# Prediction: maxima, shift and router a step sooner in a fused attention and expert kernel

## What is computed

```python
x = x + cross_attention(layernorm(x), ctx, ctx)   # 16 heads of 16, 1601 keys a batch, biases
x = x + causal_attention(layernorm(x))            # 16 heads, 64 positions a batch
x = x + experts(layernorm(x))                     # 8 experts, 256 -> 1024 -> 256, gelu
```

## Time and profile before

| what | value |
|---|---|
| median of 3 runs | 737.78 us (737.48 to 739.73) |
| the profiled execution | 738.75 us, span 736.7 us |
| granted TensorE clock, mean | 0.958 |
| TensorE busy | 668.6 us (91%) |
| VectorE busy | 498.7 us (68%) |
| ScalarE busy | 325.4 us (44%) |
| GpSimd busy | 226.2 us (31%) |

### The profile page before, as it was taken

The page is one execution under the profiler, slowest core; times in us unless marked ns, Lnnn a source line. Parts: engine busy times, 40 slices in busy tenths (PEclk is TensorE's granted clock), DMA queues, the critical chain, the costliest instruction groups (busy, mean ns, idle before and its releaser), DMA issues.

```text
span 736.7 us, 16650 instructions
## 1 busy us (share of the span) xinstructions
PE 668.6 (91%) x6576; PEld 549.2 (75%) x6584; DVE 498.7 (68%) x868; ACT 325.4 (44%) x517; POOL 226.2 (31%) x111
## 2 busy tenths in 40 slices
PE   2969999999999968999997999976897999999997
PEld 2648878878778846876885886654766898999996
DVE  4785687886748774774877757477556766676663
ACT  2434555554444533445453443445235443434431
POOL 2004566665535643643654644200000000000000
PEclk9988999999999988999998998999797999999999
DMA  6120120110110010001000000031400233112000
GB/s 227 58 68 2 25 67 24 27 44 24 25 44 24 24 26 23 23 24 46 24 24 23 2 1 2 1 116 40 189 1 1 115 115 116 69 45 114 0 0 28
DMA packets 12501, 34.16 MB, mean 46 GB/s; under 512 B 1483, under 2 KB 9812, under 8 KB 10260
## 3 DMA queue, kind: packets, MB, share of 16 engines
q1 hardware_dynamic: 12180, 31.62, 12.9%
q0 software_dynamic: 256, 1.58, 0.6%
HBM read 32.67 MB, written 0.52 MB: 45 GB/s over the span
## 4 chain that ended last, share of the span: by engine, by line
PE 79%; DVE 14%; issue 3%; ACT 2%; DMA 1%; SPq 0%; DVEq 0%; POOL 0%; ACTq 0%
PE bank L1015 44%; PE bank L1179 13%; PE bank L1024 8%; PE bank L1075 4%; DVE maxes L762 4%; PE bank L1118 2%; DVE ctx_lo L703 2%; PE bank L1109 2%; DMA bias_sb<-in_biases 1%; PE bank L1093 1%; ACT probs L638 1%; DVE shift L721 1%; DVE prob_sum L431 1%; DVE ties L810 1%; DVE masked L711 1%
## 5 line engine op out<-in xcount | busy, mean ns | idle before, releaser
L431 POOL TENSOR_TENSOR prob_sum<-probs,prob_sum 128x1024 f32<-128x1024 f32 x84 | 203.4, 2421 | 150.1 <-ACT probs L638 149.3
L638 ACT ACTIVATE probs<-bank 128x1024 f32<-128x1024 f32 (+1 forms) x104 | 106.6, 1025 | 140.4 <-PE bank L1179 137.2
L762 DVE TENSOR_REDUCE maxes<-bank 128x1 f32<-128x400 f32 (+1 forms) x256 | 131.5, 564 | 22.2 <-PE bank L1075 20.3
L620 ACT ACTIVATE h_raw<-bank,b_sb 128x512 f32<-128x512 f32 (+1 forms) x72 | 46.2, 642 | 106.8 <-PE bank L1015 106.7
L744 DVE SCALAR_TENSOR_TENSOR k_lo<-bank,bias_sb,k_hi 128x400 fp32r<-128x400 f32 (+2 forms) x64 | 40.5, 632 | 58.5 <-ACT k_hi L541 58.4
L1179 PE MATMUL bank<-qbd_hi,k_hi 64*128 64x256 f32 (+1 forms) x416 | 72.6, 343 | 7.5 <-issue 4.1
L1015 PE MATMUL bank<-w_hi,h_hi 128*128 128x256 f32 x256 | 72.9, 285 | 0.2 <-DVE h_lo L962 0.2
L1015 PE MATMUL bank<-w_hi,h_lo 128*128 128x256 f32 x256 | 72.6, 284 | 0.0
L1015 PE MATMUL bank<-w_lo,h_hi 128*128 128x256 f32 x256 | 72.5, 283 | 0.0
L961 DVE CAST h_hi<-h_raw 128x512 fp32r<-128x512 f32 (+1 forms) x72 | 28.5, 396 | 63.5 <-ACT h_raw L620 63.1
L1024 PE MATMUL bank<-probs,v_sb 128*32 128x128 f32 (+1 forms) x1664 | 69.1, 285 | 2.5 <-DVE masked L711 2.0
(11 more groups left out here) (157 smaller groups left out, 1452.2 us busy)
## 6 DMA issues: line engine op xcount, KB each, us to landing
raw<-in_w SPq DMA_DIRECT2D x16, 1024.0 KB, 6.8
ctx_raw<-in_ctx_t SPq DMA_DIRECT2D x16, 400.0 KB, 3.6
ctx_raw<-in_ctx_t SPq DMA_DIRECT2D x8, 402.0 KB, 3.6
ctx_raw<-in_ctx_t SPq DMA_DIRECT2D x8, 399.0 KB, 3.6
w_sb<-in_w_t POOLq DMA_DIRECT2D x1, 1280.0 KB, 9.5
x_all<-in_x SPq DMA_DIRECT2D x1, 512.0 KB, 3.8
w_raw<-in_w_t SPq DMA_DIRECT2D x1, 512.0 KB, 4.9
result<-x_all SPq DMA_DIRECT2D x1, 512.0 KB, 2.7
```

Source lines behind the costliest of these rows:

```text
L431: engine.tensor_tensor(prob_sum[0:ROWS[k], :], probs[0:ROWS[k], s % 2, :], acc[0:ROWS[k]], ALU.add).then_inc(summed, 1)
L620: nc.scalar.activation(h_raw[:, c % 2, 0:width], bank[:, at, 0:width], ACT.Gelu, bias=b1_sb[:, bass.ds(e, 1), c:c + 1].rearrange("p a b -> ...
L638: nc.scalar.activation(probs[0:ROWS[k], s % 2, :].rearrange("p (g n) -> p g n", g=G), bank[0:ROWS[k], 0:ROW_TILES, :], ACT.Exp, scale=SCAL ...
L762: nc.vector.tensor_reduce(maxes[:, g * PAIRS + j, c:c + 1], src[:, 0:width], AX.X, ALU.max).then_inc(read_dve, 1)
```

## The change

Three tables and one condition. The maxima of the next batch end with step 9 instead of 10: one pair fewer in step 10, one more in step 2. `find_shift` is worked at the start of VectorE's step 10 (k = KT - 3) instead of 11; X stays in step 12. In the middle tiles `y2` moves from step 19 to 18, `xt2` from 21 to 20, `router` from 22 to 21, and with them what follows on each: statistics, inverse root, normalisation, split, `row_max`, `route`. `gt` stays in step 24. Since one line is added, lines behind line 81 carry a number higher by one in the changed kernel.

```diff
-M_AT = in_order({1: 2, 2: 1, 3: 2, 4: 1, 5: 2, 6: 2, 7: 1, 8: 2, 9: 2, 10: 1})
+M_AT = in_order({1: 2, 2: 2, 3: 2, 4: 1, 5: 2, 6: 2, 7: 1, 8: 2, 9: 2})
...
 SHIFT_AT = KT - 1
+FIND_SHIFT_AT = KT - 3
...
-            15: ["o0"], 16: ["o1"], 19: ["y2"], 21: ["xt2"], 22: ["router"], 24: ["gt"], 25: ["b2"]}
+            15: ["o0"], 16: ["o1"], 18: ["y2"], 20: ["xt2"], 21: ["router"], 24: ["gt"], 25: ["b2"]}
...
-                    if k == SHIFT_AT - 1 and more > bi:
+                    if k == FIND_SHIFT_AT and more > bi:
```

## The result

The changed kernel takes **736.03 us** (median of 22 runs, 732.90 to 738.29). The kernel before, run beside it, takes 738.66 us (22 runs, 737.26 to 741.19). The ratio is 0.9959 with a 95% interval of 0.9948 to 0.9971: about 3.0 us less, where 2.0 were forecast. The interval begins and ends on the faster side, at 0.3 to 0.5%.

What follows compares the result with a forecast made beforehand. TensorE bounds the kernel, idling at gt for gates whose VectorE route GpSimd's sums hold. Middle tiles gain 2.4 us, step 3 costs 0.4: 2.0 us less, 737.78 to 735.8 us (chance 0.45), range 732.0 to 738.6.

Steps and rivals of the forecast that it cites:

- rival 1: Middle tiles: L810 wins the heat, one sum fewer holds the route; 4.6 us in all, 733.2 us; chance 0.22.
- rival 2: Middle tiles: the route meets no sum and the wait goes; 6.2 us a tile, 725.8 us; chance 0.05.
- rival 3: Middle tiles: moving ctx_lo costs what the route gains, scores of step 12 stay at 270.6; 738.2 us; chance 0.16.
- rival 4: Middle tiles: row_max comes 2.4 us late, a fourth sum holds the gates; each tile 1.2 later, 740.6 us; chance 0.12.
- The price of the pair at step 3: First pair of step 3 needs keys step 2 just made; 0.1 us in each of four batches, +0.4 us.
- the 0.29 us that the pair gives back ahead of step 10: TensorE's time for a pair of maxima ahead of step 10's scores, 0.29 us; behind scores it takes 0.18.
- The middle tiles: Route starts 3.7 us sooner, ends 1.2 us sooner after a third sum; 1.2 us a tile, 2.4 for two.
- the dead heat: Middle tiles: next sum due 4.99 us after 254.9, L810 starts 4.98 after it; taken as lost, held to 262.3.
- TensorE, slow as before: Middle tiles, from gt to X: TensorE takes 3.2 us and needs X at 268.8.
- The scores of step 12 at 269.4: Middle tiles: scores of step 12 start at 269.4 instead of 270.62, 1.2 us a tile.
- The rule of the Trainium skill: GpSimd and two-SBUF-input VectorE operations exclude each other; L815 would be held too, and rival 1 end at 735.8.
- A VectorE instruction that begins inside a sum ends when the sum does: Reading of VectorE's and GpSimd's rows: L806 takes 1.95 us and L810 2.37 inside sums, L809 0.23 between them.

Runs made afterwards that it cites:

- e2: Kernel before with only y2, xt2 and router one step sooner in the middle tiles, maxima and shift as before: 737.01 us, ratio 0.9981.
- e10: Kernel before with GpSimd's sum of step 10, second batch of middle tiles, waiting for the gate tile: 731.95 us, ratio 0.9915.
- e11: Kernel before with GpSimd's sum of step 10, second batch of middle tiles, waiting for the shift: 732.15 us, ratio 0.9906.
- e7: Changed kernel with GpSimd's sum of step 9, second batch of middle tiles, waiting for the gate tile: 730.94 us, ratio 0.9890.
- e4: Changed kernel with y2, xt2 and router another step sooner in the middle tiles (17, 19, 20): 732.65 us, ratio 0.9932.
- e8: Changed kernel with GpSimd's step 9 sum waiting for the gate tile and y2, xt2, router at 17, 19, 20: 725.65 us, ratio 0.9806.

## Why the prediction was right, and where not

- **The kind and the size.** -2.0 us were forecast, -3.0 measured; 735.8 against 736.03, inside the range of 732.0 to 738.6. (The kernel before also came out 0.9 us higher in these runs, so the ratio is the fairer measure.) That the median came out to 0.2 us is luck: the gain was 1 us larger than forecast, the kernel before 0.9 us slower than in its first runs, and inside the gain two errors work against each other, a price set too low and a gain in the middle tiles set too low. The forecast's mechanism, a route that starts sooner but meets a third sum, is what the rows show. Rivals 1 to 4 fall: not one sum fewer; the wait doesn't go; it does what it says; and exponential 9 starts at 256.83, right behind the router's and the split, with no fourth sum for the route.
- **The price of the pair at step 3: mis-sized**, +0.4 us in the forecast, 0.98 + 0.20 + 0.17 = 1.35 measured. The last of these is batch 6, which the forecast left out because `y1` lies between. The step itself was priced well: 3.59 - 3.22 = 0.37 us against 0.2 + 0.18. What was wrong is the 0.29 us that the pair gives back ahead of step 10. In batches 2 and 4 it stays (the batches are 0.14 and 0.20 us longer); in batches 0 and 1 it is lost again: step 9 is 0.28 shorter but steps 10 and 11 are 0.10 and 0.19 longer, because X there waits for a shift that hangs on the sums of steps 9 and 10: the scores of step 12 in batch 0 start 9.48 us after those of step 9 before, and 9.49 after. The forecast held that the shift would still be held by its sum, which is so (the spread L722 takes 3.19 us and ends at 100.65), and did not draw the consequence that a wait of fixed end eats what is gained ahead of it. X's wait there did not stay, it grew by the 0.19 us, from 0.74 (e2, e10, e11) to 0.93; the 0.96 of the earlier trace rows counts a missing product as idle.
- **The middle tiles: mis-sized**, 1.2 us a tile forecast, 0.72 + 1.26 = 1.98 and 0.74 + 1.15 = 1.89 measured. Up to scores 11 the working holds (0.78 forecast, 0.72 measured). From there to `gt` 5.45 us were forecast, 4.88 came. The first term that failed is the dead heat, taken as lost: the operation in question (L811 in the new numbers) started 0.06 us ahead of the second sum. That brought no sum less, since the last operation of the route met the third one; it brought a shorter tail: the last held operation is the gate tile itself, and 0.16 us follow the sum instead of 0.56. The second is "TensorE, slow as before" between `gt` and X, worth 0.25 us in batch 3: the granted clock, which before is 0.50 from 265.6 us on, ahead of `gt`, is 1.00 in the changed kernel until after `gt` and 0.50 only from 267.3. TensorE is done with the work in front of X at 267.83, 1.99 us after `gt` and not 2.89 (269.73 before), and stands still for 0.62 us of that, since the shift ends at 268.31. In batch 5 the clock falls at `gt` itself, TensorE is slow as before, and X doesn't wait.
- **The scores of step 12 at 269.4** came out to 0.01 us (269.39), by errors that cancel: TensorE was 0.8 us later at scores 11 than the forecast had it.
- **The rule of the Trainium skill** (SBUF — State Buffer, shared port pair), by which the last operation of the route would be held too: the trace agrees, L816 takes 1.98 us in the third sum and 0.17 outside one. The forecast left it aside since no row had shown it; the rule held. It is also why the won heat did not lead to rival 1. With L815 held, the forecast's working puts rival 1 not at its own 735.8 but 0.4 us a tile below it, 0.16 behind the third sum instead of 0.56, and that is what the rows show.
- **A reading that was too short.** "A VectorE instruction that begins inside a sum ends when the sum does" fits the route's operations of 0.2 us. The split of the earlier trace rows ends at 260.04, 0.86 us behind the sum's end at 259.18: it waits for the end and then does most of its own 0.98 us. The forecast's sums used the measured lengths and don't suffer.
- **What gives back:** none of the step's losses came from ScalarE; its wait for `row_max` grew by 1.7 us in total without reaching TensorE.

## What to carry to other kernels

When one engine's long operations hold up another's short ones, as GpSimd's sums did VectorE's route here, it is the order of the two that costs, not the amount: hold back the long one, whose result is wanted late, by a wait on the chain of short ones (e7, e10). Moving the short chain sooner only buys the distance to the next long operation. And an operation freed at one place moves the wait to the next in the queue: the two edits that came to 0.3 and 0.7% alone (e4, e7) came to 1.5% together (e8).

## What was not expected of the hardware

- How many two-input operations run between two sums hangs on hundredths: the gap of 0.38 us (260.31 to 260.69) let two through, the gap of 0.26 us one. A reduction over one input (L814) ran unhindered inside a sum.
- The hold works both ways: the three sums from 260.07 us in e7, between which the split and the shift each get a turn, take 8.73 us together, 2.91 each instead of 2.39.
- What is added to an operation inside a sum has nothing to do with its size: the gate tile, 8 columns and 0.17 us alone (1.98 in the third sum), and the split of 800 columns (0.99 us alone, 2.75 in the earlier trace rows) both wait for the sum's end.
- The granted clock behind one and the same 1.95 us of idleness is 1.00 in the profile of the changed kernel and 0.50 in that of e8, and the batch is 3.6 us apart.
